# Slot list in lines of 64 bytes, routing one group sooner, offsets in two banks, row clears on SyncE

## What is computed

```python
xn = _layernorm(x)
q, k, v = heads(xn @ wq.T + bq), heads(xn @ wk.T + bk), heads(xn @ wv.T + bv)     # 16 heads of 16
off = tanh(pw_w @ gelu(depthwise_conv3(q_lin) + dw_b) + pw_b) * 6.0               # 12 samples a head
positions = clip(arange(q) + linspace(-2, 2, 12) + off, 0, q - 1)
scores = (q . sample(k, positions)) / 4 - rel_scale * |positions - arange(q)|
s = (softmax(scores) @ sample(v, positions)) @ wo.T + bo
# experts: top 2 of 8 by (xn @ Wr.T + br + bias), gates normalised over the two
y = sum over the 2 chosen e of gate[e] * ((silu(a_e) * b_e) @ Wl2[e] + bl2[e]),  [a_e, b_e] = xn @ Wl1[e] + bl1[e]
out = x + s * silu(y)
```

## Time and profile before

| | |
|---|---|
| median of 3 executions | 1437.6 us (1434.17 to 1440.89) |
| profiled execution, its own time | 1440.41 us |
| its span | 1438.7 us, mean granted clock of TensorE 0.976 |
| busy in the span | TensorE 1356.0, VectorE 1223.1, GpSimd 861.8, ScalarE 802.4 us |
| DMA | 293.98 MB, mean 204 GB/s |

### The profile page before, as it was taken

The page is one execution under the profiler, slowest core; times in us unless marked ns, Lnnn a source line. Parts: engine busy times, 40 slices in busy tenths (PEclk is TensorE's granted clock), DMA queues, the critical chain, the costliest instruction groups (busy, mean ns, idle before and its releaser), DMA issues. The chain is left out here.

```text
span 1438.7 us, 35852 instructions
## 1 busy us (share of the span) xinstructions
PE 1356.0 (94%) x13687; PEld 1085.2 (75%) x13687; DVE 1223.1 (85%) x1700; ACT 802.4 (56%) x1873; POOL 861.8 (60%) x566
## 2 busy tenths in 40 slices
PE   5998999997799999999999999999999998899997
PEld 4864565556688888888888888888888886777775
DVE  7846755786899999999999999999999999999361
ACT  2547577777445455545444555545454455665664
POOL 1000377887568888778787877988887746121021
PEclk9999899998899999999999999999999999999999
DMA  7942456886747687775768577677767678999798
GB/s 226 348 166 88 105 161 201 252 258 211 250 134 214 173 233 192 224 225 150 242 141 256 142 229 192 169 223 176 212 153 214 167 169 268 250 267 228 217 275 170
DMA packets 204278, 293.98 MB, mean 204 GB/s; under 512 B 25601, under 2 KB 161029, under 8 KB 203891
## 3 DMA queue, kind: packets, MB, share of 16 engines
q0 software_dynamic: 65792, 146.59, 39.9%
q1 hardware_dynamic: 110723, 133.04, 29.3%
q10 hardware_dynamic: 27632, 12.64, 3.5%
HBM read 182.83 MB, written 117.74 MB: 209 GB/s over the span
## 5 line engine op out<-in xcount | busy, mean ns | idle before, releaser
L1398 POOL DMA_INDIRECT moe_rows<-expert_mem,token_of x142 | 363.3, 2558 | 90.3 <-issue 49.9
L1676 PE MATMUL pY<-expert_mem 128*128 x1136 | 264.2, 386 | 0.0
L1379 POOL DMA_INDIRECT expert_mem<-xn_rows,token_of x138 | 227.7, 1650 | 52.5 <-issue 45.1
L1676 PEld LDWEIGHTS pY<-expert_mem 128*128 128x128 f32 x1136 | 210.0, 190 | 41.8 <-issue 16.1
L1867 DVE SCALAR_TENSOR_TENSOR mid<-pos_pair,mid 128x768 f32<-128x768 f32 x224 | 197.6, 954 | 0.5
L1670 PE MATMUL pA<-mid,expert_mem 128*128 128x256 f32 x768 | 177.4, 385 | 4.4 <-ACT mid L1504 2.7
L1523 ACT ACTIVATE expert_mem<-pA,b1sel 128x256 f32<-128x256 f32 x284 | 111.2, 474 | 122.9 <-issue 122.7
L556 POOL DMA_INDIRECT slot_list<-token_i,high_part x128 | 141.0, 1101 | 58.2 <-issue 38.7
L1670 PE MATMUL pB<-mid,expert_mem 128*128 128x256 f32 x768 | 173.6, 379 | 0.0
L1532 ACT ACTIVATE expert_mem<-pB,b1sel 128x256 f32<-128x256 f32 x284 | 111.5, 475 | 109.2 <-PE pB L1670 109.2
L219 DVE SCALAR_TENSOR_TENSOR mid<-mid 128x768 f32<-128x768 f32 x192 | 169.6, 952 | 0.0
(11 more groups left out here) (223 smaller groups left out, 2546.6 us busy)
## 6 DMA issues: line engine op xcount, KB each, us to landing
expert_mem<-in_w_l POOLq DMA_DIRECT2D x48, 1024.0 KB, 7.7
band<-band_rows SPq DMA_DIRECT2D x256, 96.0 KB, 3.1
S_rows<-expert_mem SPq DMA_DIRECT2D x64, 376.0 KB
bandT<-in_w_l POOLq DMA_DIRECT2D x23, 1024.0 KB, 7.1
band_rows<-wgt SPq DMA_DIRECT2D x12, 1536.0 KB, 7.2
pos_pair<-pos_rows SPq DMA_DIRECT2D x28, 384.0 KB, 7.9
xn_rows<-expert_mem SPq DMA_DIRECT2D x16, 512.0 KB, 5.5
v_rows<-expert_mem SPq DMA_DIRECT2D x16, 512.0 KB, 4.3
```

Of the source, the lines that this page charges most:

```text
L1379: nc.gpsimd.indirect_dma_start(out=xs[:, u, s], out_offset=None, in_=dram["xn"], in_offset=bass.IndirectOffsetOnAxis(ap=keep["inv"][:, 2 * ...
L1398: nc.gpsimd.indirect_dma_start(out=dram["moe"], out_offset=bass.IndirectOffsetOnAxis(ap=keep["inv"][:, 2 * n + s:2 * n + s + 1], axis=0), ...
L1676: mm = nc.tensor.matmul(pY[:, s], hid[:, h, c, s * P:(s + 1) * P], w2[:, c, ds(e * D, D)], start=False, stop=(s == 1 and c == HC - 1))
```

## The change

Six things, in the front block and one wait of the second.

- The slot list in DRAM has rows of 16 float32 (64 bytes) in place of one int32. GpSimd makes the initial list in SBUF with one copy of 128 x 142 x 16 elements (in memory that keys of the second sequence use later, for which ScalarE's `evacuate_k(8)` now waits for `list_set`). The scatters write 64 bytes each, out of a float copy of the token numbers. The read back brings 1.16 MB, waits for the scores of group 13, whose keys lay there, and VectorE takes the first number of each line.
- VectorE's order: `slopes_of_k(n+2)` comes before `choose` in group 0, `count_rows` follows `choose` in group 0, and `gate_values`, `find_slots` and `experts_of_pairs` are in group 1, the first two ahead of its `offset_bias`. TensorE's `count_tokens` comes behind the first `head_scores` of group 1. ScalarE's exponent comes behind the second score tile of group 0, not the fourth.
- `pOff` has two banks, taken by turns: `offsets` waits for the addition before the last one. The counts' PSUM is part of the second bank; VectorE copies them out first (`counts_taken`).
- The clears of `moe_rows` are 16 DMAs of 0.5 MB on SyncE, one a group, behind the store of its third score tile.
- The pad clears are issued at the start, behind the initial list.
- VectorE's entry into the second block waits for 5 pads and 16 clears.

```diff
-        pOff = ps("pOff", [P, 512])
-        pCount = ps("pCount", [P, 2 * EXPERTS])
+        pOff = ps("pOff", [P, 2, 512])
+        pCount = pOff[:, 1, 2 * HR:2 * HR + 2 * EXPERTS]
...
+            def clear_moe(q):
+                sp.dma_start(dram["moe"][rows_of(q), :].rearrange("(t p) c -> p t c", p=P),
+                             zeros[:, None, :].broadcast_to([P, GROUP, D])).then_inc(moe_cleared, 16)
...
                     if a == 1 and n >= 2:
                         store_pos(n - 2)
+                    if a == 2:
+                        clear_moe(n)
...
-            pool.dma_start(dram["list"].rearrange("(p n) o -> p (n o)", p=P), spare_i[:]).then_inc(list_set, 16)
+            nc.gpsimd.tensor_copy(lines, spare_i[:].unsqueeze(2).broadcast_to([P, HIGH, LINE])).then_inc(lines_set, 1)
+            pool.wait_ge(lines_set, 1)
+            pool.dma_start(dram["list"].rearrange("(p n) l -> p n l", p=P), lines).then_inc(list_set, 16)
...
...
                         out=dram["list"], out_offset=bass.IndirectOffsetOnAxis(ap=list_row[:, c:c + 1], axis=0),
-                        in_=token_i[:, c:c + 1], in_offset=None).then_inc(scattered, 16)
+                        in_=token_f[:, c:c + LINE], in_offset=None).then_inc(scattered, 16)
...
-                clear_moe(q)
...
             pool.wait_ge(scattered, 16 * LISTED)
-            pool.dma_start(spare_i[:], dram["list"].rearrange("(p n) o -> p (n o)", p=P)).then_inc(list_loaded, 16)
+            pool.wait_ge(s_done, LINES_GROUP * GROUP + 1)
+            pool.dma_start(lines, dram["list"].rearrange("(p n) l -> p n l", p=P)).then_inc(list_loaded, 16)
...
             def offsets(n, h):
                 pe.wait_ge(gel_ready, n + 1)
-                if 2 * n + h > 0:
-                    pe.wait_ge(off_ready, 2 * n + h)
+                if 2 * n + h > 1:
+                    pe.wait_ge(off_ready, 2 * n + h - 1)
+                if 2 * n + h == 1:
+                    pe.wait_ge(counts_taken, 1)
...
                 head_scores(n, 0)
+                if n == COUNT_AT:
+                    count_tokens()
...
+                slopes_of_k(n + 2)
                 if n == 0:
                     for k in range(TOPK):
                         choose(k)
-                slopes_of_k(n + 2)
+                    count_rows()
+                if n == COUNT_AT:
+                    gate_values()
+                    find_slots()
                 if n > 0:
...
                     offset_bias(n - 1, 0)
-                if n == COUNT_AT:
-                    gate_values()
-                    count_rows()
-                if n == COUNT_AT + 1:
-                    find_slots()
```

More of the change, by code:

```diff
@@ L301, in front_block @@
         ones = sb("ones", [P, P])
+        counts = sb("counts", [P, 2 * EXPERTS])
         rows_i = sb("rows_i", [P, EXPERTS], I32)
@@ L707, in _ @@
                 evacuate_s(n, 1)
+                if n == 0:
+                    act.wait_ge(exp_in, 1)
+                    nc.scalar.activation(expw, prod, ACT.Exp).then_inc(exp_out, 1)
                 if n + 1 < STEPS:
@@ L983, in gate_values @@
             def gate_values():
-                dve.wait_ge(exp_out, 1)
-                chain(V.tensor_tensor(count, chosen[0], chosen[1], ALU.add))
                 chain(V.tensor_tensor(scores[:], expw, count, ALU.mult))
@@ L991, in count_rows @@
             def count_rows():
+                dve.wait_ge(exp_out, 1)
+                chain(V.tensor_tensor(count, chosen[0], chosen[1], ALU.add))
                 for e in range(EXPERTS):
@@ L999, in find_slots @@
                 dve.wait_ge(prefix_ready, 1)
-                chain(V.tensor_scalar(rows_i[:], pCount[:, EXPERTS:2 * EXPERTS], float(PAIR - 1), None, ALU.add))
+                V.tensor_copy(counts[:], pCount).then_inc(counts_taken, 1)
+                dve.wait_ge(counts_taken, 1)
+                chain(V.tensor_scalar(rows_i[:], counts[:, EXPERTS:2 * EXPERTS], float(PAIR - 1), None, ALU.add))
                 shift = PAIR.bit_length() - 1
@@ L1006, in find_slots @@
                 chain(V.tensor_tensor(start[:], ends[:], rows[:], ALU.subtract))
-                chain(V.tensor_tensor(start[:], start[:], pCount[:, 0:EXPERTS], ALU.add))
+                chain(V.tensor_tensor(start[:], start[:], counts[:, 0:EXPERTS], ALU.add))
                 chain(V.tensor_tensor(rank, rank, per_tile(start[:]), ALU.add))
@@ L1156, in _ @@
             dve.wait_ge(list_loaded, 16)
-            chain(V.tensor_copy(list_f[:], spare_i[:]))
-            V.tensor_scalar(keep["inv"][:], list_f[:], float(TOKENS), None, ALU.add).then_inc(tokens_known, 1)
+            V.tensor_scalar(keep["inv"][:], lines[:, :, 0], float(TOKENS), None, ALU.add).then_inc(tokens_known, 1)
             offset_bias(STEPS - 1, 0)
@@ L1978, in build @@
         "moe": nc.dram_tensor("moe_rows", [TOKENS + SPARE, D], F32).ap(),
-        "list": nc.dram_tensor("slot_list", [SLOTS, 1], I32).ap(),
+        "list": nc.dram_tensor("slot_list", [SLOTS, LINE], F32).ap(),
         "bias": nc.dram_tensor("bias_parts", [NB, EXPERTS, 2 * D], BF16).ap(),
```

50 lines of the change are left out of this document (28 added, 22 removed).

## The result

The changed kernel takes 1423.1 us at the median of 4 executions (1416.5 to 1426.5), the kernel before 1439.2 us (1434.2 to 1442.0, 4 executions beside them): a ratio of 0.9887, 95% interval 0.9867 to 0.9908, so 1.1% or 16.2 us faster. The forecast was 1421.0.

A forecast was written before the change was run, and what follows sets the result against it. It took the front's TensorE holes (routing, "issue", handover) as removable, with TensorE full in the expert pairs behind. Terms -8.9 - 3 - 7 + 1.5 = -17.4 us gave 1420.2 from the median 1437.6, stated as 1421; range 1410 to 1433.

The forecast's parts named there:

- Opening: Start of the kernel: 1.6 MB more of list and pad stores, mostly fitting in DMA room; +1.5 us, bounds 0 and +5.
- GpSimd's copy: Start of the kernel: GpSimd copies 2272 elements per partition before the list is stored, 2 to 6 us; TensorE doesn't wait.
- Routing: Front groups 1 to 3: routing one group sooner removes TensorE's waits and slow projections; -8.9 us, bounds -11 and -4.
- Middle groups: Front: clears in 0.5 MB pieces on SyncE leave fewer TensorE stops under full DMA engines; -3 us, bounds -7 and +1.
- holes by "issue": TensorE's front: 10.3 us of stops in eight places, the longest 3.1 us, read as late instructions behind full DMA engines.
- Handover: Front's end to first expert pair: list early, waits for it and for the offsets' bank go; -7 us, bounds -9.7 and -1.3.
- the list itself: End of the front: reading back 1.16 MB takes 7 us with its latency, and VectorE no longer waits for it.
- The chain: GpSimd's 128 scatters: start near 145 us, lose 6 us of clears from 186, end near 325 us against 352.9.
- Behind the first pair: Expert pairs: TensorE busy 40.00 of 40 us, so what is gained before the first pair should reach the end.
- The handover that keeps its length: Rival, entry into the pairs: VectorE enters only 1.3 us sooner, opening costs 4.8 us; -5.4 us, 1432 us; 16 in 100.
- Wider scatters: Rival, GpSimd's scatters: 64-byte elements are slower and set the first pair; 1480 us at the gather's price; 4 in 100.
- 16 clears hold up SyncE's queue: Rival, front groups: clear pieces delay score stores until ScalarE waits; two us over in each of 14 groups, 1448 us; 3 in 100.

The follow-up runs named there:

- Late_start: The changed kernel with the list's first filling and pad clears stored only when all rows are normalised, wide lines kept: 1580.7 us on a slower chip, ratio 1.0048.
- short_lines: The changed kernel with the slot list again one int32 a row, without GpSimd's copy, early pads kept: 1415.3 us, ratio 0.984 to the kernel before.
- late_short: The changed kernel with one-int32 list rows, and initial list and pads stored only when all rows are normalised: 1414.3 us, ratio 0.9848 to the kernel before.
- rep_before: The kernel before, run again without edit on the usual chip with a profile of its own: 1436.5 us.
- after_again: The changed kernel, unedited, on a chip of the slower sort: 1583.9 us beside 1573.8 for the kernel before, ratio 1.0065.
- pool_clears_again: The changed kernel with four 2 MB clears back on GpSimd between quarters of the scatters, each behind a wait for positions: 1568.0 us on a slower chip, ratio 0.9964.
- paced_short: The late_short kernel with its 128 scatters in bursts of 10, one a group: 1528.7 us on a slower chip, ratio 0.9697 to the kernel before.
- after: The changed kernel's first profiled execution, on the usual chip: 1416.5 us, the quickest of its four.
- rep_after: The changed kernel, unedited, on another chip of the slower sort: 1582.1 us beside 1571.7 for the kernel before, ratio 1.0065.
- before: The kernel before the change, in its first profiled execution: 1440.4 us.

## Why the prediction was right, and where its steps were off

The mechanisms of the routing and of the handover were right, and so was the total. That the total came so near is in part luck: the opening cost 1.5 us more than forecast and the handover gave 2.2 us less, and the other two parts made up 2.1 us of these 3.7. The shares of the parts are read from the traces: on the usual chip runs took out the wide lines and the early pads, but none took out the order of the routing, the second bank or the small clears, so that these brought the gain is argued from the rows and not isolated. Point by point, measured as the difference of this pair of traces and, in brackets, of the means of two traces of before and three with the new order in the table above.

- **Opening: +1.5 forecast, +3.0 measured.** The mechanism was another one than that priced. The forecast spread the added bytes over the DMA engines; in fact one small load beside them, the bias of q and k, landed in 12.6 us in place of 7.0, and TensorE waited 4.76 us for it. GpSimd's copy took 2.08 us, the low end of the estimate. Late_start and short_lines remove the wait.
- **Routing: -8.9 forecast, -9.7 measured (-8.1).** Each term came as priced: totals 1.16 us (1.2), the remaining holes by ScalarE 0.37 + 0.83 us (1.0), projections at 3.70 us. Both slow sets of projections that the forecast took out (6.12 and 6.19 us) are gone; the set of 5.87 us that is left is the one of 6.26 us that the forecast didn't count. In the second trace of before the same two sets took 5.39 and 5.40 us, so this part's gain depends on how long the clock stays down, and the bracketed 8.1 us is the safer number. That the same order with one bank waits 4.23 us shows that the two parts belong together.
- **Middle groups: -3 forecast, -4.3 measured (-3.2).** The holes by "issue" fell to 4.4 us, 4.8 in short_lines and 4.5 in late_short, from 10.3 and 7.3. That the small clears did it is argued, not shown. Nor was this term free to be added to the others: in the kernel before a faster middle only lengthens the wait for the list, as its second trace shows, and it counts here because the list comes sooner.
- **Handover: -7 forecast, -4.8 measured (-7.3).** VectorE's wait for the list went, as said, and ScalarE became late next, as said (5.0 us in four waits). The step mis-sized in this pair is the list itself. The first scatter started at 148.2 us, not 145, by the opening's 3.0 us alone: counted from the first scores it is 35.7 us against 35.4 forecast. The chain took 184.4 us, not 180, of which 3.1 us are scatters that took 1.126 us on average in place of 1.101 (the same with short lines, so not the width). And the wide list took 7.8 us or more to land. It was there at 343.4 us, not 332, and only because VectorE had waited 4.42 us for TensorE's offsets just before did it cost no more than 0.51 us. Late_short, whose list lands in at most 3.6 us, has 1 us less in this part.
- **Behind the first pair: nothing forecast.** The pairs keep the lead (15.8 us at the first, 16.5 at the last). The profiled execution ends 23.8 us sooner than that of before; the 7 us over are in its last part, where traces of one and the same kernel differ as much, and not in the medians, which lie 16.2 us apart.

The sum of the four measured terms is 3.0 - 9.7 - 4.3 - 4.8 = -15.8 us, against the -17.4 of the forecast, and the medians say -16.2.

**The rivals.** The handover that keeps its length is out: it was 35.9 and 39.4 us before and is 30 to 31 us. Wider scatters cost GpSimd nothing (0.971 us), nor do 16 clears hold up SyncE's queue: ScalarE has no wait for the store of scores. Two parts of the change, the wide lines and the early pads, turned out to be a cost: late_short, without them, is no slower in any part of the table and 3 us sooner at the first scores. What no rival held is the way in which the change is slower: on chips where the engines starve while GpSimd issues scatters, it takes away the waits that fed them. The holes by "issue" in the earlier trace rows may be the same thing in small: rep_before has none from 122 us to its first scatter at 164 us. The forecast read them as late instructions behind full DMA engines, and on the usual chip nothing here tells the two apart.

## What to carry to other kernels

Move one-off work such as routing to where TensorE still has other work queued, and give its consumer a second buffer in the same step: the earlier routing with one bank left a wait of 4.23 us and a slow stretch behind it. Bulk stores at the start can make a small load beside them late, so store what isn't needed yet later. Before adding up gains along a kernel, ask whether a chain on another engine ends later than all of them: by the two traces of the kernel before, it was the scatters' start, 18 us sooner, that let the other gains reach the first pair. A long chain of indirect DMAs on GpSimd should have pauses: on chips of the slower sort it cost 1.30 us a scatter in runs of 96 and 32, and 0.88 us in bursts of ten, and a wait that looks idle on GpSimd may be what lets the others run.

## What the runs showed of the hardware

- A scatter of 128 elements costs GpSimd 0.97 us and a gap of 0.30 us, with 4 or with 64 bytes an element.
- On two of four chips TensorE, VectorE and ScalarE all but stand while such DMAs are issued without a pause (on a third only the kernel before, with 1577 us, and the bursts ran): 24 matmuls in 100 us, with DMA engines 5% busy and no packet on the queues of instructions (after_again). The profile lays most of TensorE's holes to "issue". The indirect DMAs in the expert pairs do no harm (TensorE busy 40.00 of 40 us from 600 us on, in after_again as well), where TensorE runs 189 matmuls in 40 us and not 773 as in the front.
- The loss shrinks with the length of the burst: 1.30 us a scatter in runs of 96 and 32 (after_again), 1.18 us with GpSimd's waits after each quarter (pool_clears_again), 0.88 us in tens (paced_short). The three kernels differ in more than the bursts.
- After a wait of 2 to 3.4 us TensorE's granted clock was 0.55 to 0.60 over the next 6 us, and eight projections took 5.87 to 6.26 us in place of 3.70; after 0.83 us it was 1.00. In rep_before, behind the same waits, it was 0.66 to 0.76 over 5 us.
- A load of 2 KB landed in 12.6 and 13.1 us (after, rep_after) beside 1.16 MB and 0.5 MB of stores issued within 4 us of it, and in 6.4 to 7.0 us without them (before, rep_before, late_start, late_short).
- Two executions of the kernel before whose totals differ by 4 us (1440.4 and 1436.5) differ by 3 to 4 us in each of three parts, in both directions: in the first by the clock, in the last by the wait for the list (3.90 and 9.75 us).
